# A graph layer's first dense product on one Trainium2 core, computed turned for two bins at a time

## What is computed

```python
def gcn_conv(x, W, b, src, dst, n_nodes):
    h = x @ W
    deg = segment_sum(ones_like(dst), dst, num_segments=n_nodes)
    dinv = where(deg > 0, rsqrt(deg), 0.0)
    norm = dinv[src] * dinv[dst]
    msgs = h[src] * norm[:, None]
    out = segment_sum(msgs, dst, num_segments=n_nodes)
    return out + b

h = gcn_conv(_layernorm(x), W1, b1, src, dst, n)   # 100000 edges and 6250 self loops
h = relu(h)
out = gcn_conv(h, W2, b2, src, dst, n)
```

## Time and profile before

| | us |
|---|---|
| median of the runs | 3398.9 |
| the profiled execution, span from first to last instruction | 3527.4 |
| PE busy in it | 3143.9 |
| PE busy from the first turn of the first layer to its last tile (1242 us) | 1165.6 |
| POOL busy in the profiled execution | 1842.0 |

### The profile page before, as it was taken

The page is one execution under the profiler, slowest core; times in us unless marked ns, Lnnn a source line. Parts: engine busy times, 40 slices in busy tenths (PEclk is TensorE's granted clock), DMA queues, the critical chain, the costliest instruction groups (busy, mean ns, idle before and its releaser), DMA issues. The chain is left out here.

```text
span 3527.4 us, 56846 instructions
## 1 busy us (share of the span) xinstructions
PE 3143.9 (89%) x19474; PEld 2019.7 (57%) x19474; DVE 1942.6 (55%) x2983; ACT 1205.6 (34%) x1447; POOL 1842.0 (52%) x1754
## 2 busy tenths in 40 slices
PE   7237999999999999967999999999999998588998
PEld 7125666666666666634665656665656664244665
DVE  8773444444443444425777877777777775101332
ACT  6951222222222222213444444444444442011000
POOL 0146666666666666536676666776666661100000
PEclk9999999999999999979999999999999999799999
DMA  9488888888888888749998988988889987999996
GB/s 374 180 316 317 293 280 287 303 287 271 298 284 299 293 295 297 263 159 312 313 307 291 311 298 297 312 302 294 288 286 308 308 284 287 340 324 271 277 268 177
DMA packets 344441, 1018.61 MB, mean 289 GB/s; under 512 B 145314, under 2 KB 148668, under 8 KB 335984
## 3 DMA queue, kind: packets, MB, share of 16 engines
q0 software_dynamic: 135776, 660.85, 56.5%
q1 hardware_dynamic: 196916, 322.85, 27.3%
q10 hardware_dynamic: 11484, 31.39, 2.8%
HBM read 854.14 MB, written 135.08 MB: 280 GB/s over the span
## 5 line engine op out<-in xcount | busy, mean ns | idle before, releaser
L1299 POOL DMA_INDIRECT xs<-table,idx x833 | 914.2, 1097 | 501.3 <-PE m_part L1476 214.0
L821 POOL DMA_INDIRECT xs<-table,idx x833 | 878.8, 1055 | 442.9 <-issue 202.9
L1073 PE MATMUL a_part<-xs 128*128 128x512 f16 (+1 forms) x3332 | 592.1, 332 | 76.1 <-DMA xs<-table,idx 52.5
L1476 PE MATMUL m_part<-xs 128*128 128x512 f16 (+1 forms) x3332 | 591.9, 332 | 55.7 <-DMA xs<-table,idx 19.2
L1053 PE MATMUL a_ps_o<-Ws,xs 128*128 128x512 f16 x3528 | 593.1, 326 | 8.9 <-issue 5.5
L1073 PEld LDWEIGHTS a_part<-xs 128*128 128x128 f16 x3332 | 416.3, 142 | 213.2 <-issue 96.9
L1476 PEld LDWEIGHTS m_part<-xs 128*128 128x128 f16 x3332 | 419.3, 142 | 198.4 <-issue 77.3
L1053 PEld LDWEIGHTS a_ps_o<-Ws,xs 128*128 128x128 f16 x3528 | 344.9, 98 | 236.8 <-issue 12.6
L1505 PE MATMUL m_ps_l<-xs,m_xT 128*128 128x512 f16 x1764 | 391.6, 380 | 8.0 <-issue 7.9
L1492 PE MATMUL m_ps_s<-dw_mem,xn_mem 128*128 128x512 f16 x1296 | 312.2, 380 | 3.5 <-DVE xs L1365 3.0
L1505 PEld LDWEIGHTS m_ps_l<-xs,m_xT 128*128 128x128 f16 x1764 | 172.2, 98 | 219.2 <-issue 16.8
(11 more groups left out here) (377 smaller groups left out, 3770.9 us busy)
## 6 DMA issues: line engine op xcount, KB each, us to landing
xs<-in_L_ffn_w_dram SPq DMA_DIRECT2D x64, 1152.0 KB, 11.3
xs<-table SPq DMA_DIRECT2D x98, 384.0 KB
xs<-table,idx POOLq DMA_INDIRECT x1666
cw_dram<-xs SPq DMA_DIRECT2D x49, 512.0 KB
x_pad<-xs SPq DMA_DIRECT2D x7, 2688.0 KB, 23.9
table<-arena SPq DMA_DIRECT2D x49, 384.0 KB, 4.5
table<-xs SPq DMA_DIRECT2D x49, 384.0 KB
xs<-x_pad SPq DMA_DIRECT2D x49, 384.0 KB
```

Of the source, the lines that this page charges most:

```text
L821: pool.indirect_dma_start(out=ring[:, t, :], out_offset=None, in_=table, in_offset=bass.IndirectOffsetOnAxis(ap=idx[:, k:k + 1], axis=0)). ...
L1073: mm = nc.tensor.matmul(part[:, bass.ds(to + a, z - a)], pick[:, i % 2, :, t], ring[:, n % RING, half * D + a:half * D + z], start=False, ...
L1299: pool.indirect_dma_start(out=ring[:, t, :], out_offset=None, in_=table, in_offset=bass.IndirectOffsetOnAxis(ap=idx[:, n:n + 1], axis=0)). ...
L1476: mm = nc.tensor.matmul(part[:, bass.ds(off + at, e - f)], pick[:, i % 2, :, t], ring[:, n % RING, half * D + f:half * D + e], start=False ...
```

## The change

The first product is computed turned and for a pair of bins at once: a 128x128 block of W1 is stationary, and the turned sums of two bins (256 columns of `vT`) move. Its result already has features on the partitions and nodes in the columns, which is what the second product needs, so `h2`, the turn of h and the two copies to `hT` are gone. The product of a pair falls into six units of 18 matmuls (one for each 128 features of the result), three in the iteration behind the pair's second bin and three in the next. A unit's result (256 columns of `ps_o`) is read by DVE (bias from a column, factor from a row, in one operation), ACT forms the high half with a ReLU and DVE the low half. The factors are needed as rows: they are turned once, stored to a small table in memory and loaded for each pair by SP. The second product comes one iteration later, the ring has 14 rows instead of 16, and `vT`, the factor rows and the scratch lie in the freed rows.

```diff
-        RING = CT - 1
+        PW = 2 * P
+        RING = CT - 3
...
+        def pair_units(i):
+
+            m, first = ((i - 1) // 2, 0) if i % 2 else ((i - 2) // 2, DC // 2)
+            return [(m, c) for c in range(first, first + DC // 2)] if 0 <= 2 * m < NBR else []
...
@@ sync
+                    if i >= 2 and i % 2 == 0:
+                        m = (i - 2) // 2
+                        wait(sp, h_read, DC * m)
+                        for q in pair_bins(m):
+                            b = own_block(sp, tab, q)
+                            sp.dma_start(fac_rows[:, P * (q % 2):P * (q % 2) + P], fac_dram[bass.ds(b, 1), :].to_broadcast([P, P])).then_inc(fac_in, 16)
...
@@ scalar
+                def hidden(m, c):
+                    n = P * len(pair_bins(m))
+                    act.wait_ge(h_read, DC * m + c + 1)
+                    nc.scalar.activation(hT[m % 2][0][:, c, 0:n], t_h[:, c % 2, 0:n], ACT.Relu).then_inc(ht_hi, 1)
...
@@ vector
+                def hidden(m, c):
+                    n, k = P * len(pair_bins(m)), DC * m + c
+                    v.wait_ge(prod1, k + 1)
+                    v.wait_ge(fac_in, 16 * pair_bins(m).stop)
+                    wait(v, ht_lo, k - 1)
+                    v.scalar_tensor_tensor(t_h[:, c % 2, 0:n], ps_o[:, D:D + n], bcol[:, c:c + 1], fac_rows[:, 0:n], ALU.add, ALU.mult).then_inc(h_read, 1)
+                    v.wait_ge(ht_hi, k + 1)
+                    v.scalar_tensor_tensor(hT[m % 2][1][:, c, 0:n], t_h[:, c % 2, 0:n], 0.0, hT[m % 2][0][:, c, 0:n],
+                                           ALU.max, ALU.subtract).then_inc(ht_lo, 1)
...
-                    j = i - 2
+                    j = i - 3
...
-                        v.scalar_tensor_tensor(u[:, :], ps_o[:, 0:D], inv[:, 0:1], brow[:, :], ALU.mult, ALU.add).then_inc(biased, 1)
-                        v.wait_ge(biased, i + 1)
-                        v.tensor_scalar(tmp[:, :], u[:, :], dinv_s2[:, bass.ds(b, 1)], 0.0, ALU.mult, ALU.max).then_inc(h_f, 1)
-                        v.wait_ge(h_f, i + 1)
-                        v.wait_ge(h_hi, i + 1)
-                        v.tensor_tensor(h2[:, 1, :], tmp[:, :], h2[:, 0, :], ALU.subtract).then_inc(h_lo, 1)
...
@@ tensor
+                def hidden(m, c):
+                    n = P * len(pair_bins(m))
...
+                    wait(pe, h_read, DC * m + c)
+                    for d in range(DC):
+                        for half, Wp in ((0, W1s[0]), (0, W1s[1]), (1, W1s[0])):
+                            mm = nc.tensor.matmul(ps_o[:, D:D + n], Wp[:, d, c * P:(c + 1) * P], vT[:, half, d, 0:n],
+                                                  start=(d == 0 and half == 0 and Wp is W1s[0]), stop=(d == DC - 1 and half == 1))
+                    mm.then_inc(prod1, 1)
...
+                    def unit(n):
+                        if pair_units(i - 1):
+                            m, c = pair_units(i - 1)[n]
+                            wait(pe, t_lo, min(i - 3, NBR))
+                            hidden(m, c)
...
+                    if 0 <= i - 4 < NBR:
+                        wait(pe, h_read, DC // 2 * (i - 2))
+                        second(i - 4)
...
+                    if i % 2 == 0:
+                        steps(3, 5)
...
+                            turn(i - 1)
+                        steps(5, 9)
...
+                        unit(0)
+                        steps(9, 12)
+                        unit(1)
+                        steps(12, 15)
+                        unit(2)
+                        steps(15, CT)
+                    else:
+                        unit(0)
+                        steps(3, 6)
+                        unit(1)
+                        steps(6, 9)
+                        unit(2)
+                        steps(9, 13)
...
+                            turn(i - 1)
+                        steps(13, CT)
```

More of the change, by code:

```diff
@@ L794, in _ @@
             def _(sp):
-                for i in range(NBR + 4):
+                for i in range(NBR + 5):
                     if i < NBR:
@@ L879, in _ @@
                         nc.scalar.activation(norm, ps_s[:, 0:K], ACT.Sqrt).then_inc(rooted, 1)
[L880 to L887, removed]
+                    if i % 2 == 1 and i < NBR:
+                        turned_high(i)
+                    for m, c in pair_units(i):
+                        hidden(m, c)
                     if i < NBR:
                         phi_parts(i)
-                        act.wait_ge(biased, i + 1)
-                        wait(act, h_turned, i)
-                        nc.scalar.activation(h2[:, 0, :], u[:, :], ACT.Relu, scale=dinv_s2[:, bass.ds(b, 1)]).then_inc(h_hi, 1)
+                    if i % 2 == 0 and i < NBR:
+                        turned_high(i)
             @block.vector
@@ L1002, in _ @@
                         wait(v, v_hi, i)
[L1003 removed]
+                        wait(v, v_lo, i)
                         v.wait_ge(based, 2 * i + 2)
@@ L1022, in _ @@
                         choose(i + 2)
-                    if i + 1 < NBR:
+                    if i % 2 == 1 and i < NBR:
+                        turned_low(i)
+                    if i % 2 == 1 and i + 1 < NBR:
                         add_own_rows(i + 1)
[L1025 to L1032, removed]
+                    for n, (m, c) in enumerate(pair_units(i)):
+                        hidden(m, c)
+                        if i % 2 == 0 and n == 0 and i + 1 < NBR:
+                            add_own_rows(i + 1)
+                    if i == 0:
+                        add_own_rows(1)
                     if i < NBR:
@@ L1050, in product, with second @@
+                def second(j):
+                    m, at = j // 2, P * (j % 2)
+                    pe.wait_ge(ht_hi, DC * (m + 1))
+                    pe.wait_ge(ht_lo, DC * (m + 1))
+                    wait(pe, t_lo, j)
+                    if j == 0:
+                        pe.wait_ge(lo2, 1)
                     for c in range(DC):
-                        for half, Wp in ((0, Ws[0]), (0, Ws[1]), (1, Ws[0])):
+                        for half, Wp in ((0, W2s[0]), (0, W2s[1]), (1, W2s[0])):
@@ L1052, in product @@
                             for a, z in ((0, 512), (512, D)):
-                                mm = nc.tensor.matmul(ps_o[:, a:z], turned_rows[:, half, c * P:(c + 1) * P], Wp[:, c, a:z],
-                                                      start=(c == 0 and half == 0 and Wp is Ws[0]), stop=(c == DC - 1 and half == 1))
-                    return mm
-                def turn(rows):
+                                mm = nc.tensor.matmul(ps_o[:, a:z], hT[m % 2][half][:, c, at:at + P], Wp[:, c, a:z],
+                                                      start=(c == 0 and half == 0 and Wp is W2s[0]), stop=(c == DC - 1 and half == 1))
@@ L1058, in turn @@
+                    mm.then_inc(prod2, 1)
+                def turn(i):
+                    pe.wait_ge(v_lo, i + 1)
+                    wait(pe, vt_hi, i)
+                    wait(pe, vt_lo, i)
                     for half in range(2):
                         for c in range(DC):
-                            mm = nc.tensor.transpose(ps_t[:, half, c * P:(c + 1) * P], rows[:, half, c * P:(c + 1) * P], ident16[:, :])
-                    return mm
-                for i in range(NBR + 3):
+                            mm = nc.tensor.transpose(ps_t[:, half, c * P:(c + 1) * P], v2[:, half, c * P:(c + 1) * P], ident16[:, :])
+                    mm.then_inc(v_turned, 1)
@@ L1064, in steps @@
+                for i in range(NBR + 4):
                     def steps(first, last):
@@ L1123, in _ @@
[L1123 to L1132 removed]
+                            pe.wait_ge(fac_r, 1)
+                        if 0 <= i - 1 < NBR:
+                            turn(i - 1)
```

126 lines of the change are left out of this document (70 added, 56 removed).

## The result

| | before | after |
|---|---|---|
| median of six runs each | 3395.65 us (3392.09 to 3399.05) | 3408.31 us (3405.31 to 3411.58) |
| profiled execution: time, span | none, 3527.4 us | 3411.58, 3409.8 us |

The ratio is 1.0034, 95% interval 1.0024 to 1.0045. The change costs 12.7 us where 16 were to be gained.

A forecast was written before the change was run, and what follows sets the result against it. PE was taken to bound the first layer (busy 1165.6 of 1242 us). With prompt signals, 22.5 pairs x (-1.34 + 0.3) + 7 = -16, so 3398.9 - 16 = 3383 us; range 3360 to 3435, the forecast's own 3370 to 3400.

The forecast's parts named there:

- Prompt signals in the timed runs: PE's completion signal arrives 0.2 us after the work, not 2.0, in runs without a profile: -16 us, chance 0.42.
- the 128.5 us: Timed median of before, 3398.9 us, lies this far (3.6%) under its profiled span of 3527.4; ascribed to waits when profiled.
- The first rival: Signals 2.0 us late in timed runs too, also at the units: 3408 to 3450 us, middle 3430, chance 0.33.
- (1): Turn of h on PE goes: 0.67 us a bin, plus 1.3 us of wait before it if signals are late.
- (2): First product as 256-column matmuls on PE: 0.108 us each, no change; at most 0.22 us more a bin.
- The rival of dear matmuls: 256-column matmuls on PE cost more than half a 512-wide one: 1.2 us a bin, +58 us, 3457; chance 0.03.
- (3): Units on PE wait for DVE's read of the result buffer: hidden when prompt, 0.6 us at each unit when late.
- (4): First unit of an odd iteration waits for the second product's eviction: 0.3 us a pair prompt, 2.1 late.
- (5): DVE loses 3.2 us a bin and gains 2.7, ACT swaps copy and Relu for three short Relus; neither on the path.
- (6): Ring shrinks from 16 rows to 14: POOL's gathers, 23.0 us a bin against PE's 23.4, still keep up; no cost.
- (7): Pipeline one bin deeper: tail 17 us longer, 10 us gained in iterations 1 and 3; net +7, bounds +5 and +17.
- the -10 at the start: Iterations 1 and 3 have one product fewer on PE, 11.7 us, of which 10 were counted as gained.

The follow-up runs named there:

- experiment 1: Both kernels unaltered, run again with profiles: before 3520.07 us on one chip and 3392.02 on another; after 3411.71, 3406.19 and 3410.24 us.
- experiment 4: Changed kernel with the three units of odd iterations two tiles later and the turn one tile later: 3401.32 us, ratio 1.0013 to the kernel before.
- experiment 2: Kernel before with a ring of 14 rows instead of 16, nothing else changed: ratio 0.9999 on each of two chips.
- experiment 5: Changed kernel with 36 idle matmuls (5.85 us of PE) added at the start of iteration 3: 3405.73 us, ratio 1.0025 to the kernel before.

## Why the prediction was wrong

It said 3383 us, faster; it is 3408.31, slower by 0.34%. The mechanism in the steady bins held and the ends were mis-sized.

- **Prompt signals in the timed runs: right**, and for a wrong reason. I put the 128.5 us down to the profiled execution; experiment 1 shows that they belong to the chip. Span and time of one execution differ by 1.8 us (3390.2 and 3392.02). The prediction also took the 128.5 us as evidence against a figure for a profile and its own execution; they are none, since they compare two chips. The first rival (late, 3408 to 3450) contains the result by coincidence: its waits are not in the profile of after.
- **(1) The turn of h**: 0.67 us and no wait with prompt signals, as computed.
- **(2) 256 columns**: 18 take 925.91 to 927.87, 0.109 us each, within the bounds; 0.09 us more a pair than my value, for 108 starts in place of 72. The rival of dear matmuls falls. The Trainium skill (TensorE: Matmul & The Clock Gate, section "Wait — 56ns, not 53.3ns?") gives columns over 2.4 GHz plus some 2.5 ns, which is 0.109 for 256; the trace agrees with it, and not with the sustained figures that the prediction weighed.
- **(3) Waits for h_read**: DVE's read takes 0.479 us, estimated at 0.48, and all are hidden in the steady bins.
- **(4) The new wait for t_lo**: 0.34 us a pair, forecast 0.3; experiment 4 takes it away. With (1) and (2) most pairs gain 0.92 us (48.20 to 47.28), and the sixteen of bins 16 to 48 gain 0.94 on average, forecast 1.04.
- **(5) "Neither is on the path": wrong, by 3.5 us.** Two of the four reciprocals for the mixture's weights, 1.75 us each, now stand behind the last unit of an even iteration and ahead of the next bin's first operation:

```profile
602.71 1.75 DVE L1003 RECIPROCAL xs<-xs 128x256 f32<-128x256 f32 x1
605.90 0.96 DVE L1058 TENSOR_TENSOR xs<-a_part,a_base 128x768 f32<-128x768 f32 x1 [1.45 <-issue]
```

The second product ends at 608.35 on PE, but the tiles start at 609.49, and the unit behind them another 0.6 us late. The two pairs with them take 49.05 us instead of 47.28. In before, the same reciprocal has 4.3 us of idle time behind it, ahead of L1040. This is read from the traces; no run moved the reciprocals.
- **(6) The ring: right** (experiment 2). POOL was held by PE for 114.1 us after, so gathers never bound a steady bin.
- **(7) The ends: the step that failed.** Forecast +7 with bounds of +5 and +17; they cost +24.8 in the profiles compared, and the other profiles of after give +2.6 to +6 for the start and +18.9 to +25.4 for the tail. The work and waits of the tail were forecast well (52 us; from the second product behind the last tile, 1409.84, to the end of the last L1072 it is 52.8), though not the lower clock that adds 6 us in half of the profiles. But the -10 at the start was not there. The prediction took two products fewer as time gained; the time went into the zeroing of `part`, the clock and gathers that are late, of which I had seen one and allowed 1.7 us for. In bin 2 PE even waits for gathers where before it did not, which the prediction did not have and no run explains. With the measured +6 in place of the -10 the sum of -16 is 0.

So the layer loses 8.2 us in the profiles compared: -20.7 (22 pairs by 0.94), +3.5, +6.0, +18.8 make +7.6.

Open is the **mixture**, whose instructions are the same: 614.5 to 618.4 us in the four profiles of after, 608.4 and 611.5 in two of before, 611.1 to 618.3 in the variants. Of the 10 us in the two profiles compared some 5 are waits of PE for the experts' weights from memory, 55.9 us after and 50.5 before:

```profile
PE e_pe L1976 <- DMA xs<-in_L_ffn_w_dram: 46.1, 6, 17.8
PE e_ph L1956 <- DMA xs<-in_L_ffn_w_dram: 9.8, 2, 5.4
```

```profile
PE e_pe L1894 <- DMA xs<-in_L_ffn_w_dram: 45.1, 6, 17.0
PE e_ph L1874 <- DMA xs<-in_L_ffn_w_dram: 5.4, 1, 5.4
```

These waits are 55.9 to 58.3 us in the four profiles of after, 50.5 and 52.6 in the two of before, and 52.2 in that of experiment 4, whose mixture takes 611.1 us. Another part is PE's clock: in one stretch of 100 us it was granted 0.95 before and 0.91 after. These are the rows by stretch, before and after:

```profile
2950.00:3050.00 100.00, 87.78 (x638) 47.03 (x637) 6.18 (x8) 17.46 (x22) 9.79 (x20) 0.95 1.10 324
```

```profile
2960.00:3060.00 100.00, 85.48 (x585) 45.52 (x583) 5.35 (x7) 17.47 (x22) 9.80 (x20) 0.91 1.12 303
```

Why, no run tells, nor how much of the 12.7 us in the median is the mixture's: the first layer alone is longer than before by 4.9, 8.2, 14.1 and 14.8 us in the four profiles of after.

## What to carry to other kernels

A gain of 2% in every pass through a pipelined loop is worth little beside one pass more of fill and drain: cost the first and the last iterations wait by wait, as carefully as the middle, and count a product taken from an unfilled pipeline as a gain only if nothing else is late there. Where a loop drains, give late producers the memory that is free by then; that turned the loss of this change into none, and with two more tiles of cover behind the product a gain of 11.4 us. Before costing a wait, take a trace from the kind of chip on which the kernel is timed.

## What the hardware did that was not expected

- Two chips differed by 3.9% for one program: 3528.54 and 3396.24 us are medians of the same kernel. On the first, signals of PE arrive 2.0 us behind the work in part of the bins, on the others 0.2; why stays open.
- The execution recorded here takes hardly longer than the others: 3411.58 with a profile, 3405.31 to 3411.53 without. In experiment 1 it is the other way round, 3520.07 against a median of 3528.54.
- The tail of after, the same instructions with the same waits, takes 56 us at a granted clock of 0.99 and 62 us at 0.83 to 0.85, where PE worked at 1.2 GHz for part of it. The four profiles of after fell two and two, and experiments 4 and 5, with the same tail, had 60.7 and 61.8 us at 0.86. The longest wait ahead of the lower clock is 2.1 us. So short waits between short products can cost twice, once by themselves and once by the clock.
